# A three-layer cross network on one NeuronCore: the last add of the fold moved to GpSimd, the sums over d split into two row tiles and issued later, the top layers of three groups run at once, and the opening reordered

## The reference

```python
x0 = xk = e                                        # [512, 39, 16]
for W in (f0, f1, f2):                             # [39*39,128], [39*128,128], [39*128,128]
    z = einsum('bfd,bgd->bfgd', x0, xk).reshape(b, f * g, d)
    xk = einsum('bpd,pm->bmd', z, W); outs.append(xk)
z = sum(concatenate(outs, axis=1), axis=-1)        # [512, 384], summed over d
h = relu(concat(z, dense_ctx) @ W_top1 + b_top1)   # 400 -> 512
h = relu(h @ W_top2 + b_top2)                      # 512 -> 256
y = h @ W_top3                                     # 256 -> 1
```

## Time and profile before

| | us |
|---|---|
| median of 3 runs | 706.79 |
| the profiled execution | 704.92 |
| its span | 702.8 |
| TensorE busy | 652.7 (93%) |
| VectorE busy | 593.7 (84%) |
| GpSimd busy | 504.6 (72%) |
| ScalarE busy | 389.7 (55%) |

### The profile page before, as it was taken

The page is one execution under the profiler, slowest core; times in us unless marked ns, Lnnn a source line. Parts: engine busy times, 40 slices in busy tenths (PEclk is TensorE's granted clock), DMA queues, the critical chain, the costliest instruction groups (busy, mean ns, idle before and its releaser), DMA issues.

```text
span 702.8 us, 11554 instructions
## 1 busy us (share of the span) xinstructions
PE 652.7 (93%) x2990; PEld 510.8 (73%) x2990; DVE 593.7 (84%) x2014; ACT 389.7 (55%) x1162; POOL 504.6 (72%) x465
## 2 busy tenths in 40 slices
PE   0288899999999999999999999999999999999997
PEld 0256677777777787778867777787877778787867
DVE  3569799999999898989689898989689898988660
ACT  0446465747565564657466565657456474746421
POOL 5738979796989887878579887886668786563220
PEclk9999999999999999999999999999999999999989
DMA  9527421303040303131030302112040302100000
GB/s 202 94 69 250 132 65 39 80 16 100 6 111 7 110 8 99 20 82 34 14 100 8 109 9 74 43 52 66 4 111 6 106 11 68 40 1 1 0 1 0
DMA packets 70259, 41.26 MB, mean 59 GB/s; under 512 B 47297, under 2 KB 55041, under 8 KB 70066
## 3 DMA queue, kind: packets, MB, share of 16 engines
q1 hardware_dynamic: 57010, 35.37, 18.6%
q10 hardware_dynamic: 7936, 3.88, 3.1%
q0 software_dynamic: 5248, 1.29, 1.9%
HBM read 38.55 MB, written 1.94 MB: 58 GB/s over the span
## 4 chain that ended last, share of the span: by engine, by line
PE 81%; DVE 8%; POOL 3%; issue 3%; DMA 2%; SPq 2%; ACT 1%; DVEq 0%; POOLq 0%; ACTq 0%
PE y L805 19%; PE y L807 18%; PE y L806 18%; DVE scaled L703 6%; PE side L812 5%; PE acc L787 4%; PE late L823 4%; PE acc L781 4%; PE acc L782 3%; PE y L823 2%; PE late L834 1%; DMA emb_singles<-in_tbl_dram,ids_sb 1%; PE late L866 1%; SPq L372 1%; PE side L772 1%
## 5 line engine op out<-in xcount | busy, mean ns | idle before, releaser
L703 DVE SCALAR_TENSOR_TENSOR scaled<-y,x_rows,scaled 128x128 f32<-128x128 f32 x1728 | 468.1, 341 | 63.9 <-ACT scaled L536 31.6
L536 ACT ACTIVATE scaled<-y,x_rows 128x128 f32<-128x128 f32 x768 | 219.0, 367 | 167.5 <-PE y L807 166.0
L805 PE MATMUL y<-w_hi,x_parts 128*128 128x512 f32 (+1 forms) x640 | 277.2, 433 | 4.0 <-DVE x_parts L679 3.2
L806 PE MATMUL y<-w_lo,x_parts 128*128 128x512 f32 (+1 forms) x640 | 249.2, 389 | 0.0
L807 PE MATMUL y<-w_hi,x_parts 128*128 128x512 f32 (+1 forms) x640 | 249.1, 389 | 0.0
L440 POOL TENSOR_TENSOR z_parts<-z,z_parts 117x512 fp32r<-117x512 f32 (+1 forms) x107 | 138.6, 1295 | 46.1 <-ACT z_parts L490 45.3
L429 POOL DMA_INDIRECT emb_quads<-in_small_tables_dram,quad_rows x144 | 138.6, 962 | 25.2 <-issue 13.7
L805 PEld LDWEIGHTS y<-w_hi,x_parts 128*128 128x128 f32 x640 | 120.5, 188 | 39.9 <-DVE scaled L703 13.2
L807 PEld LDWEIGHTS y<-w_hi,x_parts 128*128 128x128 f32 x640 | 120.2, 188 | 26.3
L806 PEld LDWEIGHTS y<-w_lo,x_parts 128*128 128x128 f32 x640 | 121.0, 189 | 19.7
L448 POOL TENSOR_TENSOR sum<-scaled 128x512 f32<-128x512 f32 x64 | 82.7, 1292 | 63.4 <-DVE x_sb L711 54.7
(11 more groups left out here) (84 smaller groups left out, 375.4 us busy)
## 6 DMA issues: line engine op xcount, KB each, us to landing
z<-x_turned SPq DMA_DIRECT2D x320, 78.0 KB
x_three<-x_turned SPq DMA_DIRECT2D x48, 78.0 KB
x_turned<-emb_quads SPq DMA_DIRECT2D x160, 8.0 KB
w_sb<-in_w_dram SPq DMA_DIRECT2D x1, 2496.0 KB, 9.3
emb_quads<-in_small_tables_dram,quad_rows POOLq DMA_INDIRECT x144, 2.3
s_sb<-in_w_dram ACTq DMA_DIRECT2D x12, 160.0 KB, 5.9
x_turned<-emb_singles SPq DMA_DIRECT2D x96, 2.0 KB
x_turned<-emb_quads SPq DMA_DIRECT2D x48, 6.0 KB
```

Of the source, the lines that this page charges most:

```text
L536: done = act.activation(scaled[:, k % 2, BY_ACT.index(j), i * M:(i + 1) * M], y2[n % RING][:, i * M:(i + 1) * M], ACT.Copy, scale=x0_rows[ ...
L703: dve.scalar_tensor_tensor(part, y2[n % RING][:, i * M:(i + 1) * M], x0_f, part, ALU.mult, ALU.add).then_inc(terms_in, 1)
L805: pe.matmul(dst, x1_hi[:, t % 2, cols], hi, start=True, stop=False)
L806: pe.matmul(dst, x1_hi[:, t % 2, cols], lo, start=False, stop=False)
```

## The change

- **x2.** The last add (256 to 128 columns) is done by GpSimd in `fold_three`, right behind the other two; VectorE's `x2_of` is gone but for the very last block.
- **Sums over d.** S_LAG goes from 18 to 25: `s_block` stands in slots 5, 15, 25 and 35. In all but slot 15 (and in tiles 0 and the tail) it is cut into two matmuls of 64 partitions and 160 columns, the second into another PSUM bank: `acc0` in slot 5, `three_ps` in slots 25 and 35. That is 45 of the 64 blocks. ScalarE copies each half by itself. `contract` of chunk 0 (slot 8) waits for the copy out of `acc0`; `rows_of`, now in slot 27, waits for the copy of slot 26.
- **Chunks.** Their places are 0, 4, 7, 11, 14, 18, 21 (before 0, 4, ..., 24); x1 is read from slot 31 (before 34). In tile 0 the chunks stand one slot earlier.
- **Top layers** of groups 0 to 2 run once, with 384 columns, in tile 15 (slots 13 to 37); before, each ran in tiles 7, 11 and 15 with 128.
- **Opening.** ScalarE's queue waits for the ids before it loads filters; f1 is loaded in two halves, the second after ScalarE's queue has stored its 6 of tile 0's 22 rows; two of the four roundings of f1 and `rows(0)` move among the chunks of tile 0, one low part of f1 goes to GpSimd; the other ids are loaded by SyncE in tile 0, and VectorE adds their offsets in slot 6 of tile 1 (14 instructions). The five single gathers of group 1 move from the opening and tile 0 to slots 28 of tile 0 to 0 of tile 1.

The diff, cut to its core (top-layer bodies change only in shapes and in the two banks `late` and `acc0` that they alternate between):

```diff
-X2_AT = 5
...
-B_STEP = 4
-FIRST_B_AT = 11
-FIRST_STEP = 3
...
+CHUNKS_AT = (0, 4, 7, 11, 14, 18, 21)
+FIRST_CHUNKS_AT = (10, 13, 16, 19, 22, 25, 28)
...
-X1_AT = 34
-FIRST_X1_AT = 37
-S_LAG = 18
+X1_AT = 31
+FIRST_X1_AT = 36
+S_LAG = 25
...
-ROWS_AT = 33
+ROWS_AT = 27
 THREE_AT = 38
-FIRST_THREE_AT = 10
+FIRST_THREE_AT = 9
...
-L3_AT = 10
-L3_SLOTS = 122
-H1_AT = 137
-H2_AT = 143
...
+L3_AT = 17
+L3_SLOTS = 113
+H1_AT = (133, 137, 141, 145)
+H2_AT = (150, 153)
+Y_AT = 157
...
+HALVES = (0, 20, F)
+W1_CUTS = (0, 10, 20, 30, F)
+W1_EARLY = 2
+REST_AT = 6
...
+def second_half(k):
+    t, s = divmod(k * BANKS + S_LAG, SLOTS)
+    if t == 0 or t == TILES:
+        return None
+    return "acc0" if s < BANKS else "three_ps" if s > 2 * BANKS else None
...
-    cuts = (0, 0, 0, 3, len(SINGLES))
+    cuts = (0, 0, 0, 0, len(SINGLES)) if g == 1 else (0, 0, 0, 3, len(SINGLES))
...
+                stores(u, (0,) if u == 0 else (0, 1))
...
+                    sp.dma_start(ids_sb[:, 1:GROUPS, :], ids[P:B, :].rearrange("(g p) f -> p g f", p=P)).then_inc(rest_ids_in, 16)
+                    for j in range(4):
...
+                if u == TILES - 1:
+                    sp.wait_ge(three_up, TILES - 1)
+                    sp.wait_ge(rows_t, TILES - 1)
                     sp.dma_start(dense_sb[:, :], dense_t).then_inc(top_in, 16)
...
+            def second_filter_low(i):
+                cut = slice(W1_CUTS[i], W1_CUTS[i + 1])
+                pool.wait_ge(w1_hi_in, i + 1)
+                pool.tensor_tensor(w1_lo[:, cut, :], w1_raw[:, cut, :], w1_hi[:, cut, :].bitcast(F32),
+                                   ALU.subtract).then_inc(w1_lo_pool, 1)
...
+                if g == 1 and i == 0:
+                    pool.wait_ge(rest_ids_in, 80)
...
+                if u == TPG and i == 0:
+                    pool.wait_ge(quads_rest, 1)
...
                 pool.tensor_tensor(sum2[:, :], sum4[:, 0:2 * M], sum4[:, 2 * M:4 * M], ALU.add).then_inc(two_in, 1)
+                pool.wait_ge(two_in, k + 1)
+                if k >= 2:
+                    pool.wait_ge(s_ready, k - 1)
+                pool.tensor_tensor(x2_sb[:, k % 2, :], sum2[:, 0:M], sum2[:, M:2 * M], ALU.add).then_inc(x2_in, 1)
...
-            pool.wait_ge(rest_ids_in, 80)
-            pool.wait_ge(quads_rest, 1)
+            second_filter_low(W1_EARLY + 1)
...
+                if u > 2:
+                    act.wait_ge(s_in, NBLK * (u - 2) + 2)
...
-                copy(s_sb[:, g % 2, :, at:at + BLK],
-                     side[:, 0:BLK * FS].rearrange("p (b f) -> p f b", f=FS)).then_inc(s_in, 1)
+                if second_half(k) is None:
+                    copy(s_sb[:, g % 2, :, at:at + BLK],
+                         side[:, 0:BLK * FS].rearrange("p (b f) -> p f b", f=FS)).then_inc(s_in, 1)
+                else:
+                    copy(s_sb[:, g % 2, :, at:at + HALF],
+                         side[:, 0:HALF * FS].rearrange("p (b f) -> p f b", f=FS))
+                    src = {"acc0": acc0, "three_ps": three_ps}[second_half(k)]
+                    copy(s_sb[:, g % 2, :, at + HALF:at + BLK],
+                         src[:, 0:HALF * FS].rearrange("p (b f) -> p f b", f=FS)).then_inc(s_in, 1)
...
+            act.wait_ge(ids_in, 16)
...
-            for j in range(W1_PIECES):
-                load_filter(act, j)
...
+            load_filter(act, 0)
             act.wait_ge(w0_sum, 1)
             copy(w0_hi[:, :, :], w0_raw).then_inc(w0_hi_in, 1)
-            for j in range(W1_PIECES):
-                act.wait_ge(w1_in[j], 64)
-                copy(w1_hi[:, j:F:4, :], w1_raw[:, j:F:4, :]).then_inc(w1_hi_in, 1)
+            store_singles(act, 0, (1,))
+            for i in range(len(QUADS)):
+                if any(len(rows) > 1 for _, _, _, rows in runs(QUADS[i])):
+                    store_quad(act, 0, i, (1,))
+            load_filter(act, 1)
+            act.wait_ge(w1_in[0], 256)
+            for i in range(W1_EARLY):
+                high_filter(i)
             three(0)
+            rows(0)
             for c in range(C0):
                 high_part(0, c)
-                if c == 4:
-                    rows(0)
+                if c == 1:
+                    act.wait_ge(w1_in[1], 256)
+                if c in (1, 2):
+                    high_filter(W1_EARLY + c - 1)
             x1_high(0)
             act.wait_ge(mask_in, 1)
...
-            quad_numbers(slice(0, 2)).then_inc(quads_first, 1)
+            quad_numbers(slice(0, TPG)).then_inc(quads_first, 1)
...
-            dve.wait_ge(rest_ids_in, 80)
-            quad_numbers(slice(2, TILES)).then_inc(quads_rest, 1)
-            second_filter_low(W1_PIECES - 1)
...
             x1_low(0)
+            second_filter_low(W1_EARLY)
             sum_x1(0)
...
-                    if s % BANKS == X2_AT and n > BANKS:
-                        x2_of(n // BANKS - 1)
+                    if t == 1 and s == REST_AT:
+                        dve.wait_ge(rest_ids_in, 80)
+                        quad_numbers(slice(TPG, TILES)).then_inc(quads_rest, 1)
...
                 if c == 0 and u > 0:
                     pe.wait_ge(r1_in, u)
+                if c == 0 and u > 1:
+                    pe.wait_ge(s_in, NBLK * (u - 1) - 1)
                 pe.wait_ge(z_hi_in, n + 1)
                 pe.matmul(acc0[:, :], w0_hi[0:k, c, :], z_hi[0:k, s, :], start=c == 0, stop=False)
...
+                if n < BANKS:
+                    pe.wait_ge(w1_hi_in, sum(1 for at in W1_CUTS[:-1] if at <= f[-1]))
+                    pe.wait_ge(w1_lo_in, sum(1 for at in W1_CUTS[:W1_EARLY + 1] if at <= f[-1]))
+                    if f[-1] >= W1_CUTS[W1_EARLY + 1]:
+                        pe.wait_ge(w1_lo_pool, 1)
...
-                pe.matmul(side[:, 0:BLK * FS], x2_sb[:, k % 2, :],
-                          diag[:, k // NBLK % 2, k % NBLK, :, :].rearrange("p b f -> p (b f)"),
-                          start=True, stop=True).then_inc(s_ready, 1)
+                spread = diag[:, k // NBLK % 2, k % NBLK, :, :].rearrange("p b f -> p (b f)")
+                half = HALF * FS
+                if second_half(k) is None:
+                    pe.matmul(side[:, 0:BLK * FS], x2_sb[:, k % 2, :], spread, start=True, stop=True).then_inc(s_ready, 1)
+                else:
+                    t = (k * BANKS + S_LAG) // SLOTS
+                    if second_half(k) == "three_ps":
+                        pe.wait_ge(prod, C0 * min(t + 2, TILES))
+                    else:
+                        pe.wait_ge(r1_in, t + 1)
+                    to = {"acc0": acc0, "three_ps": three_ps}[second_half(k)]
+                    pe.matmul(side[:, 0:half], x2_sb[0:P // 2, k % 2, :], spread[0:P // 2, 0:half], start=True, stop=True)
+                    pe.matmul(to[:, 0:half], x2_sb[P // 2:P, k % 2, :], spread[P // 2:P, half:2 * half],
+                              start=True, stop=True).then_inc(s_ready, 1)
...
+                if c == 1:
+                    pe.wait_ge(s_in, ((TILES - 1) * SLOTS + BANKS - S_LAG) // BANKS)
+                if c >= 2:
+                    pe.wait_ge(h1_in, c - 1)
                 cut = slice(c * P, (c + 1) * P)
...
+                dst = top_bank[c % 2][:, 0:LEFT]
+                for i, x in enumerate((r1_sb, r2_sb, r3_sb)):
+                    pe.matmul(dst, wt1_sb[:, i, cut], x[:, 0:LEFT], start=i == 0, stop=False)
+                pe.matmul(dst, wt1_sb[0:16, 3, cut], dense_sb[:, 0:LEFT], start=False, stop=True).then_inc(h1_ready, 1)
...
+            rows_of(0)
             for c in range(C0):
                 contract(0, c)
-                if c == 4:
-                    rows_of(0)
-                elif c < C0 - 1:
...
             pe.wait_ge(rows_in, 1)
-            pe.wait_ge(w1_hi_in, W1_PIECES)
-            pe.wait_ge(w1_lo_in, W1_PIECES)
...
                     if t + 1 < TILES and s == ROWS_AT:
-                        if t > 0:
-                            pe.wait_ge(s_in, NBLK * t + 2)
-                        else:
-                            pe.wait_ge(s_in, 2)
+                        pe.wait_ge(s_in, NBLK * t + 1)
                         rows_of(t + 1)
...
+                    if g == GROUPS - 1:
+                        x = q * SLOTS + s
+                        if x in H1_AT:
+                            top1(H1_AT.index(x))
+                        if x in H2_AT:
```

More of the change, by code:

```diff
@@ L158, in chunk_at @@
 def chunk_at(u, s, lag):
-    step = FIRST_STEP if u == 1 else B_STEP
     if u == 1 and lag == CONTRACT_LAG:
         lag = FIRST_CONTRACT_LAG
-    c = s - lag - (FIRST_B_AT if u == 1 else 0)
-    return c // step if u < TILES and c >= 0 and c % step == 0 and c // step < C0 else None
+    places = FIRST_CHUNKS_AT if u == 1 else CHUNKS_AT
+    return places.index(s - lag) if u < TILES and s - lag in places else None
 def x1_at(u):
@@ L280, in cross_network @@
         last_h1 = (acc0, three_ps, late, y2[1])
+        top_bank = (late, acc0)
         ids_in = sem("ids_in")
@@ L287, in cross_network @@
```

(26 more changed lines are left out.)

184 lines of the change are left out of this document (102 added, 82 removed).

## The result

The changed kernel takes **715.6 us** (median of 4 runs, 712.0 to 715.7) against 707.7 for the kernel before beside it (701.8 to 709.6): ratio 1.0087, 95% interval 1.0046 to 1.0128. It is slower by .9%, within my case's 1% and its own range of 702 to 716, 5.6 us above the 710 that I gave.

What follows compares the result with a forecast made beforehand. TensorE, busy 93% of the span, was taken to bound the kernel. Terms -16 + 14 + 6 + 7 - 4 + 2 - 3 - 2 = +4 on 706.8 gave 710.8, stated as 710 us; 8-in-10 range 692 to 721.

Steps and rivals of the forecast that it cites:

- my case: Main forecast for the whole kernel: 710 us, within 1% of the kernel before, own range 702 to 716, chance .40.
- Waits that go: TensorE's waits before the sum and VectorE's lag at tile starts end: -16 us, bounds -23 and -8.
- Chunk 0: TensorE waits 1.0 us for ScalarE's copy out of `acc0` in tiles 1 to 14: +14 us.
- `rows_of`: In slot 27 TensorE waits .4 us for the copy of slot 26, in 15 tiles: +6 us, 0 to +9.
- The split: Sum over d in two row tiles costs .15 us more a block, 45 blocks: +7 us, ends -12 and +18.
- rival four: Slower: the two halves of the sum do not overlap, +11 us, 721 us; chance .17.
- rival one: Faster: row tiles run side by side, a block costs -.27 us instead of +.15, 691 us; chance .12.
- GpSimd in tile 1, +2, and the additions, 0: In tile 1, GpSimd's extra gathers cost +2 us (0 to +4); VectorE's 14 additions equal the removed x2: 0.
- Top layers once, -4: Running three groups at once with 384 columns saves only changeovers and waits: -4 us, -5 to -2.
- Opening -3, tile 0 -2: Opening: earlier row stores, -3 us (-6 to +2). Tile 0: earlier chunks and x1, fewer gathers, -2 (-4 to 0).
- Rival two: Faster: banks already hold TensorE in slots 7, 8 and 27, so +20 us shrinks to 2, 692 us; chance .18.
- rival three: Slower: GpSimd's low part of chunk 6 is late for slot 29 in some 11 tiles, +14, 724 us; chance .13.

Runs made afterwards that it cites:

- e10: Changed kernel without halves and with the additions in the opening, top layers again by group with 128 columns: 697.6 us, ratio .9920.
- e8: Changed kernel without halves and with the additions in the opening, x2's last addition back on VectorE: 694.3 us, ratio .9865.
- r2: Changed kernel without halves and with the additions in the opening, run again as base for two others: 691.6 us, ratio .9833.
- e3: Changed kernel with only the slot 5 sum whole, halves kept for blocks that go to `three_ps`: 701.4 us, ratio .9897.
- e9: Changed kernel without halves, additions in the opening, x2 of the first seven blocks on VectorE, later ones on GpSimd: 688.8 us, ratio .9789.
- e1: Changed kernel with all ids loaded early and VectorE's 14 offset additions in the opening, not tile 1: 709.0 us, ratio 1.0016.
- r1: Changed kernel unaltered, run once more on another chip: 707.4 us (11 runs), ratio 1.0061.
- third set: Last group of follow-up runs, on its own chip: r1, r2, e9 and e10, with the kernel before beside them at 703.6 us.

## Why the prediction was right, and where not

The time came out in my case's own range, but half of the terms were mis-sized, and two errors of about 10 us cancelled, which was luck: the waits that go gained some 10 less than I gave them, and the three new costs (chunk 0, `rows_of`, the split) came to 17 in place of 27.

- **Waits that go, -16: the step that failed most.** I took tile 2's 2.7 us over the sum of its instructions for waiting, and 1.0 to 1.4 in the others. TensorE's own row before the sum was 5.6 us in 14 places (above); I had chosen the weight loads' 21.4 and noted that loads run ahead, and then priced by the tile all the same. e10, with all of this and without halves, has tiles 2 to 14 except 7 and 11 only 5.5 shorter than before, `rows_of`'s wait in it. Tile 2 without halves still takes 37.0, 2.2 over the 34.8 of my sum, and its waits make up only some .7 of that: most of the 2.7 is spacing that no wait explains. Nor is VectorE's own time "worth nothing beyond this": with the sum as late and x2 back on VectorE, tiles 2 to 14 are 4.1 longer (e8). TensorE's row for VectorE's banks (4.5 against r2's 2.9) holds 1.6 of it; where the rest lies is open.
- **Chunk 0, +14:** mechanism right, in 14 places, 9.9 by its row. e3's 10.2 has 13 split blocks in it; without them (1.3) it is 8.9 in 13 tiles. I took 1.0 a tile; it is .7. ScalarE's first copy started 2.53 after slot 6's first matmul (254.85), its second .18 behind, not .30.
- **`rows_of`, +6:** 2.6 in 9 places, .9 of it in tile 0.
- **The split, +7:** .10 a block where I took .15, 4.5 in all. The halves run side by side, so rival four is out; what is lost ahead of the block and behind it is more than they gain, so rival one is too. The split sum took .47 from its first start to the next instruction's, not the .7 that I named, and under the .5 that I had called a sign of being wrong: I had put the changeover inside it, and it lies ahead of it and behind it.
- **GpSimd in tile 1, +2, and the additions, 0: the second failure.** x2 on GpSimd costs 2.2 there (e9). The additions cost 5.1 (e1), 2.7 without the halves: I set them equal to the x2 that went, by their 2.08 us in the opening, where only gathers and no tensor operation of GpSimd ran beside them. The earlier trace rows said what happens elsewhere, and I had used it for x2 in the same text.
- **Top layers once, -4:** -6.0 (e10), of which some 1.5 may be the clock.
- **Opening -3, tile 0 -2:** on record +1.9, with the hole, and -2.5 without it (r1, on another chip); tile 0 -1.0.
- **The clock** had no term. Its share was .983 in three of the four runs on record (715.6 us) and .990 in the fourth (712.0); on the third set's chip, without the hole and with .995 in most runs, the changed kernel is 3.8 us above the kernel before, not 7.9.
- **The other signs.** Tiles 5, 7 and 11 and the tail came as said. Tile 2 took 37.8 in place of near 37, and VectorE was busy 571 us in place of about 560.

Rival two (waits covered) and rival three (GpSimd late in 11 tiles) are out: chunk 0 waits everywhere, and in tiles 2 to 14 of the changed kernel TensorE never waits as much as .1 us for a low part. Rival five (the split not run as row tiles) is out, since both halves start together.

In sum: sums later and x2 on GpSimd gain some 6 in the steady tiles (4 of them by x2, e8), top layers once 4 to 6, the opening 2 to 3 where the hole is absent; the halves lose 13, the additions 3 to 5, x2 in tile 1 2. Without the halves, the additions early and the first seven x2 on VectorE (e9), the rest of the change is worth 2.1%.

## What to carry to other kernels

Price a removed wait by the bounding engine's own row before that instruction, never by the gap between a tile's length and a sum of instruction times. Before moving many small VectorE operations with two SBUF inputs into a busy stretch, look for GpSimd operations there: one of them can stand behind two. And a short matmul cut into row tiles has to win back what it loses on both sides, and a bank that its half borrows can bring a wait for the copy out of it: here `acc0` did, .7 a tile, and `three_ps` did not.

## What the runs showed of the hardware that was not expected

- Row tiles of 64 start 7 ns apart at most in all 90 pairs (both at 254.14 above), yet pairs follow each other .24 us apart, the spacing of a 512-column matmul, at 160 columns. A sum in two halves costs .10 to .13 us more than the whole one.
- The lower clock level costs in steps: among the changed kernel's 11 runs of the third set, nine have a mean granted clock of .995 and take 706.1 to 708.4 us, two have .990 and take 711.5 and 711.6. The low stretches that I followed in the profiles came behind an idle TensorE. But the same wait of 3.13 us in tile 1 was followed by a mean clock of .92 over that tile on record and .96 in r1, 45.3 us against 43.6; what decides between them no run here shows.
- In the hole, TensorE's last transpose ended at 30.50 and ScalarE's copy of it began at 35.59, while the core's transfers ran at 72 GB/s in place of 196:

```profile
30.00:36.00 6.00, 0.49 (x5) 0.32 (x4) 1.00 (x2) 0.41 (x2) 2.31 (x3) 0.71 0.28 72
```
```profile
30.00:36.00 6.00, 4.88 (x20) 2.79 (x18) 4.52 (x8) 4.54 (x8) 4.47 (x4) 1.00 0.66 196
```

The first is the changed kernel on record, the second the same kernel in the third set.
